# The first attention's output norm moved from VectorE to GpSimd (three of four batches), with a new order of stages

## The chip, the cores and the metric

The kernel runs on one core of a Trainium2 chip. The metric is the device time of one execution in microseconds (us). PE is TensorE, DVE is VectorE, ACT is ScalarE, POOL is GpSimd, SP is SyncE; PEld is the loading of weights into PE.

## What is computed

Three blocks in a row on an input of 4 batches, 64 channels and 32 x 32 places (1024 tokens). The first is the one that the change touches:

```
x_ln = layernorm over channels(x);  q, k, v = 4 heads of 16
attn = softmax(q k^T / 4);  out = attn v                   # 1024 x 1024 a head
x  = x + proj(out) + b
x  = x + fc2(gelu(fc1(layernorm(x))))
```

The second is an attention with 8 heads over a sliding window of 32 tokens, the third a recurrence `y = sigmoid(Wx + V y)` along the 1024 tokens behind a norm over all tokens. The three together make the result.

## The kernel before, in words

**Tiling.** A batch lies as 128 partitions (64 channels x 2 halves of 512 tokens). The first attention runs in 256 score tiles (`scores`: 4 batches, 16 units, 4 heads), each one bf16 matmul of 512 columns on PE (line 815), one exponential on ACT (line 1146) and, for every four of them, a `values` step of eight fp32 matmuls of 32 weight columns (line 830). The maximum that the softmax subtracts is found beforehand: 256 `max_piece` tiles, each one bf16 matmul on PE (line 795) and one reduction over 512 columns on DVE (line 1308). Scores and max pieces share a ring of PSUM banks (`plan_ring`): a matmul waits until ACT or DVE has read what its bank held.

**The norm.** A `values` tile carries, beside the outputs of a head, the sum of its exponentials. At the end of each half DVE copies the bank (`values`, line 1340) to `o_sb`, SP spreads the sums by DMA to `den_sb`, ACT computes `rden = exp(-log(den))` (`den`, line 1153, and `den_exp`, line 1159), and stage `o_norm` improves it by one Newton step and multiplies, in three DVE instructions a half (lines 1348, 1350 and 1352): `step = den*rden`, `step = (2 - step)*rden`, `o_norm = o_sb*step`. `proj` (line 852) on PE waits for the semaphore `o_normed` of each half, and `fc1`, `fc2`, layer norms and the whole second attention of that batch follow. The last batch (`apart`) reads its sums from PSUM and keeps buffers of its own. `o_norm` and `hid`, the hidden layer between `fc1` and `fc2`, are one buffer.

**The order.** Each engine runs its own instructions in the order of one list of stages, `order_of_stages`. The host of the list is `scores` and `values` of the four batches. `MAX_AT` says behind how many of these host stages each max piece goes, `LAYER_AT` does so (in quarter steps) for all other stages of the batches before, `END_AT` and `UNIFY_AT` for the end. So the tables set what stands ahead of what in every queue. POOL runs `split` (the parts of q and k of batches 1 to 3, which SP then sends through DRAM to the layout that scores need) and `round_query` (casts of the second attention's queries).

Of the kernel before, what the change touches and what calls it, by code (L numbers as in the profile page):

```python
# [8 lines left out]
ALU = mybir.AluOpType  # L9
# [134 lines left out]
def attend_stages(b):  # L144

    out = []
    for u in range(UNITS):
# [11 lines left out]

MAX_AT = (  # L160
    (
        0, 0, 0, 0, 1, 1, 1, 6, 6, 7, 8, 8, 10, 10, 11, 12, 13, 15, 15, 15, 15, 16, 21, 21, 21, 21, 21, 22, 24, 29, 34),
    (
        39, 39, 39, 39, 46, 46, 48, 48, 49, 51, 51, 51, 53, 55, 55, 55, 58, 59, 60, 61, 61, 63, 63, 68, 68, 68, 68,
        71, 71, 73, 74, 76, 76, 79, 79),
    (
        80, 80, 80, 83, 83, 83, 84, 85, 86, 86, 86, 86, 98, 99, 100, 101, 101, 101, 101, 103, 105, 105, 105, 105, 105,
        106, 107, 107, 107, 107, 107, 107, 109, 110, 112),
    (
        112, 114, 114, 116, 116, 116, 116, 117, 117, 117, 118, 119, 120, 122, 122, 125, 125, 127, 127, 136, 136, 137,  # L170
        137, 137, 137, 138, 143, 143, 146, 146, 147, 147, 147, 149, 151),
    (
        154, 155, 157, 157, 160, 163, 163, 163, 164, 167, 168, 169, 170, 171, 172, 172, 172, 181, 181, 185, 185, 185,
        185, 185, 186, 186, 187, 188, 188, 188, 189, 190, 190, 191, 191),
    (
        191, 193, 194, 196, 196, 196, 196, 197, 197, 197, 197, 198, 198, 198, 198, 198, 202, 208, 216, 221, 221, 221,
        222, 222, 222, 223, 223, 224, 224, 229, 229, 232, 233, 234, 234),
    (
        234, 237, 237, 239, 239, 240, 240, 242, 242, 242, 243, 243, 244, 254, 255, 255, 255, 257, 257, 257, 258, 258,
        260, 261, 261, 262, 262, 262, 266, 266, 267, 268, 271, 271, 271),  # L180
)
LAYER_AT = (
# [72 lines left out]
def build(nc, a, out):  # L255

    with ExitStack() as ctx:
        def sb(name, shape, dt=F32):
            return ctx.enter_context(nc.sbuf_tensor(name, shape, dt))

        def sem(name):
            return ctx.enter_context(nc.semaphore(name))
# [15 lines left out]
        for n in ("w1q", "w1k", "w1v", "w1u"):  # L278
# [45 lines left out]
        o_sb = sb("o_sb", [P, 2, HALF])  # L324
# [3 lines left out]
        o_norm = sb("o_norm", [P, 2, HALF])  # L328
# [50 lines left out]
            ln_ctr ln_sq ln_var ln_log ln_rstd ln_norm  # L379
            bias_mm bias_done fold_mm fold_done qk_mm v_mm qk_hi qk_rst qk_mid qk_lo qk_dram qk_in v_copied  # L380
            max_mm max_red negmax negmax_t mx_h mx_r mx_m mx_done shift_in
            st_mm exp_done pv_mm o_copied den_in den_mm den_log rden_done den_prod rden_new o_normed proj_mm x1_done
            fc1_mm gelu_done fc2_mm x2_done
            xp_pad xbd_cast z_mm z_copied z_moved z_cast z_cast_odd tok_mm tok_copied
            sel_zero sel_done lay_mm lay_in lay_in2
# [5 lines left out]
        g = {n: sem(n) for n in names}  # L391


        def half_rows(h):
            return slice(h * C, (h + 1) * C)
# [60 lines left out]
        def pair(b):  # L456
            return T[:, 0:2, :] if apart(b) else R[:, 0:2, :]
# [184 lines left out]
        @block.gpsimd  # L642
        def _(pool):


            nc.gpsimd.memset(eps[:], 1e-5).then_inc(g["pool_fills"], 1)
            nc.gpsimd.memset(sel, 0.0).then_inc(g["sel_zero"], 1)
            for i in range(2):
                nc.gpsimd.memset(VT[i][:], 0.0).then_inc(g["pool_fills"], 1)
            pool.wait_ge(g["pool_fills"], 3)  # L650
            for i in range(2):
                nc.gpsimd.memset(VT[i][:, :, :, HD:HP], 1.0).then_inc(g["pool_fills"], 1)
            nc.gpsimd.memset(den_sb[:], 1.0)
            nc.gpsimd.memset(xp[:], 0.0)
            nc.gpsimd.memset(xbd16[:], 0.0).then_inc(g["pool_fills"], 1)
            for i in range(2):
                pool.wait_ge(g["pool_fills"], 6 + i)
                nc.gpsimd.memset(KX[i][KQ:KQ + PARTS, :, :, :], 1.0).then_inc(g["pool_fills"], 1)
            pool.wait_ge(g["pool_fills"], 8)

            def round_query(b, h):
                n = b * H1 + h
                if b == B - 1:
                    if h % 2:
                        return
                    n = b * H1 + h // 2
                pool.wait_ge(g["z_copied"], b * H1 + h + 1)
                if n:
                    pool.wait_ge(g["z_cast"], n)
                if b and h == 0:  # L670
                    pool.wait_ge(g["fin_mm"], b)
                nc.gpsimd.tensor_copy(*z_cast_of(h)).then_inc(g["z_cast"], 1)  # L672

            def split(b):
                if b == 0:
                    return
                for half in range(2):
                    pool.wait_ge(g["qk_rst"], 2 * b + half + 1)
                    nc.gpsimd.tensor_copy(mid_rows[:, half, :], qk_rest[:, half, :]).then_inc(g["qk_mid"], 1)
                for half in range(2):  # L680
                    pool.wait_ge(g["qk_mid"], 2 * b + half + 1)
                    last = nc.gpsimd.tensor_tensor(lo_rows[:, half, :], qk_rest[:, half, :], mid_rows[:, half, :], ALU.subtract)
                last.then_inc(g["qk_lo"], 1)

            run({"round_query": round_query, "split": split})
            pool.wait_ge(g["unit_sel_done"], 1)
            nc.gpsimd.memset(v_cross, 0.0).then_inc(g["cross_zero"], 1)
            pool.wait_ge(g["cross_zero"], 1)
            nc.gpsimd.tensor_copy(v_cross[half_rows(0), half_rows(1)], t["v_rec"][half_rows(0), half_rows(0)]).then_inc(g["cross_done"], 1)
# [562 lines left out]
        def _(dve):  # L1252
# [88 lines left out]

            def o_norm_(b, half):

                if half == 0:
                    dve.wait_ge(g["rden_done"], b + 1)
                n = 2 * b + half + 1
                _, first, step = (x[:, half, :] for x in recip_bufs(b))
                TT(step, dens(b)[:, half, :], first, ALU.mult).then_inc(g["den_prod"], 1)
                dve.wait_ge(g["den_prod"], n)
                STT(step, step, 2.0, first, ALU.subtract, ALU.mult, reverse0=True).then_inc(g["rden_new"], 1)  # L1350
                dve.wait_ge(g["rden_new"], n)
                TT(o_norm[:, half, :], o_sb[:, half, :], step, ALU.mult).then_inc(g["o_normed"], 1)
# [266 lines left out]
```

## Time and profile before

| | us |
|---|---|
| median of 3 runs | 460.96 |
| lowest, highest | 454.33, 461.22 |
| the profiled execution | 458.44 |
| its span, first to last instruction | 456.5 |
| PE busy | 413.2 |
| DVE busy, ACT busy | 296.7, 296.3 |
| POOL busy | 42.3 |

The time of the profiled execution has 1.94 us around its span. Busy time is a union over an engine's instructions; that of PE is modelled from pipelined matmuls and so stands above its true use.

### The profile page before, as it was taken

What the parts mean: (1) busy time and instruction counts of PE and PEld (TensorE: products, weight loads), DVE (VectorE), ACT (ScalarE), POOL (GpSimd) and SP (SyncE); (2) the same over time, 40 slices, a digit from 0 to 9 for tenths busy, and PEclk for the clock granted to TensorE, in tenths of its full rate; (3) what the DMA queues carried; (4) which work ended last, traced back from release to release, by engine and by line L of the source; (5) the groups of instructions that cost most, each with busy time, mean ns of one, the idle gap of its engine ahead of it and who ended that gap; (6) DMA issues with size and microseconds to landing.
All of it is one profiled execution on the core that took longest, in us unless ns stands there. A gap on an engine that the chain in (4) does not pass through costs nothing.

```text
span 456.5 us, 7908 instructions
## 1 busy us (share of the span) xinstructions
PE 413.2 (91%) x3210; PEld 156.6 (34%) x3210; DVE 296.7 (65%) x541; ACT 296.3 (65%) x512; POOL 42.3 (9%) x57
## 2 busy tenths in 40 slices
PE   6787999999999999999999999899999988897893
PEld 2335232322322433232224433232134322453492
DVE  1696795989998746579885556997042644625424
ACT  3442577758788477587876675779977756264551
POOL 9300110003003000012031000000300000100000
PEclk9997699999999999999999999999999999799997
DMA  7300065001810000005500000000000000000003
GB/s 294 99 1 1 3 130 79 12 2 23 183 16 1 14 1 1 1 13 128 81 3 13 1 1 3 12 2 1 1 3 1 0 1 0 3 1 2 1 1 93
DMA packets 7158, 14.02 MB, mean 31 GB/s; under 512 B 1872, under 2 KB 4176, under 8 KB 6992
## 3 DMA queue, kind: packets, MB, share of 16 engines
q1 hardware_dynamic: 7120, 13.50, 12.7%
q8 instruction: 26, 0.43, 0.4%
q14 instruction: 12, 0.10, 0.1%
HBM read 9.20 MB, written 3.41 MB: 28 GB/s over the span
## 4 chain that ended last, share of the span: by engine, by line
PE 63%; ACT 15%; DVE 13%; issue 3%; DMA 3%; POOL 2%; SPq 1%; DVEq 0%; ACTq 0%; POOLq 0%
PE O L830 10%; PE T L815 5%; DVE part_max L1308 5%; PE T L795 5%; ACT z L1169 4%; PE R L815 3%; PE R L727 3%; PE R L999 3%; PE R L886 3%; PE R L795 3%; PE R L960 3%; PE R L721 2%; PE R L987 2%; DMA KX<-qk_scratch 2%; PE R L974 2%
## 5 line engine op out<-in xcount | busy, mean ns | idle before, releaser
L1308 DVE TENSOR_REDUCE part_max<-T 128x1 f32<-128x512 f32 x164 | 105.7, 683 | 23.4 <-PE T L795 23.1
L1146 ACT ACTIVATE probs<-T 128x512 f32<-128x512 f32 x146 | 81.3, 601 | 23.4 <-PE T L815 23.1
L1146 ACT ACTIVATE probs<-R 128x512 f32<-128x512 f32 x110 | 62.2, 599 | 19.2 <-PE R L815 18.9
L830 PE MATMUL O<-probs,VT 128*32 128x512 f32 x512 | 67.6, 603 | 0.3 <-ACT probs L1146 0.2
L1308 DVE TENSOR_REDUCE part_max<-R 128x1 f32<-128x512 f32 x92 | 60.7, 683 | 10.0 <-PE R L795 9.5
L795 PE MATMUL T<-KX,QX 96*128 96x512 bf16 x164 | 57.0, 393 | 4.6 <-DVE part_max L1308 3.0
L815 PE MATMUL T<-QX,KX 99*128 99x512 bf16 x146 | 49.6, 384 | 1.8 <-DVE part_max L1308 1.3
L815 PE MATMUL R<-QX,KX 99*128 99x512 bf16 x110 | 38.1, 382 | 0.6 <-DVE qk_rest L1285 0.4
L672 POOL CAST zs<-z 128x512 bf16<-128x512 f32 x28 | 17.2, 614 | 200.6 <-ACT z L1169 200.6
L795 PE MATMUL R<-KX,QX 96*128 96x512 bf16 x92 | 32.7, 387 | 1.8 <-DMA KX<-qk_scratch 0.9
L1177 ACT ACTIVATE p<-R 128x1024 f32<-128x1024 f32 x14 | 14.3, 1024 | 26.7 <-PE R L960 26.7
L795 PEld LDWEIGHTS T<-KX,QX 96*128 96x128 bf16 x164 | 15.0, 99 | 47.8 <-DVE part_max L1308 18.6
L1169 ACT ACTIVATE z<-R 64x512 f32<-64x512 f32 (+1 forms) x44 | 26.2, 596 | 5.6 <-PE R L886 4.6
L815 PEld LDWEIGHTS T<-QX,KX 99*128 99x128 bf16 x146 | 12.6, 97 | 38.1 <-ACT probs L1146 12.5
L1430 DVE TENSOR_TENSOR zs<-R,rden 128x512 f32<-128x512 f32 x24 | 15.4, 685 | 13.4 <-PE R L987 13.4
L1104 ACT ACTIVATE ln_q<-R 128x512 f32<-128x512 f32 (+1 forms) x14 | 8.2, 589 | 20.6 <-PE R L721 20.6
L886 PE MATMUL R<-xp,abd 64*64 64x512 f32 x128 | 17.2, 613 | 2.4 <-ACT z L1169 2.1
L1184 ACT ACTIVATE rlog<-R 128x1024 f32<-128x1024 f32 x16 | 16.3, 1020 | 4.7 <-PE R L974 4.6
L830 PEld LDWEIGHTS O<-probs,VT 128*32 128x32 f32 x512 | 10.3, 108 | 26.4 <-issue 15.8
L1400 DVE TENSOR_REDUCE neg_m<-R 128x16 f32<-128x576 f32 x16 | 12.1, 758 | 10.5 <-PE R L921 10.5
L815 PEld LDWEIGHTS R<-QX,KX 99*128 99x128 bf16 x110 | 9.7, 97 | 24.5 <-issue 6.4
L727 PE MATMUL R<-ln_q,s_first 128*128 128x512 f32 (+1 forms) x28 | 16.1, 660 | 2.1 <-ACT ln_q L1104 2.1
(241 smaller groups left out, 592.8 us busy)
## 6 DMA issues: line engine op xcount, KB each, us to landing
qk_scratch<-qk_part SPq DMA_DIRECT2D x12, 192.0 KB, 3.0
zs<-early SPq DMA_DIRECT2D x1, 2048.0 KB, 8.4
QX<-qk_scratch SPq DMA_DIRECT2D x6, 256.0 KB, 5.4
KX<-qk_scratch SPq DMA_DIRECT2D x6, 256.0 KB, 5.7
result<-probs SPq DMA_DIRECT2D x2, 512.0 KB, 5.1
s_rest<-rest SPq DMA_DIRECT2D x1, 946.0 KB, 11.1
X<-x SPq DMA_DIRECT2D x2, 384.0 KB, 12.6
QX<-qk_scratch SPq DMA_DIRECT2D x6, 128.0 KB, 5.5
```

Source lines behind the costliest of these rows:

```text
L672: nc.gpsimd.tensor_copy(*z_cast_of(h)).then_inc(g["z_cast"], 1)
L727: mm(ln_bank(b, which, i, 1), t["mean_c"], ln_bufs(b, which, i)["ln_q"], start=True, stop=True).then_inc(g["ln_var"], 1)
L795: mm(ring["max_piece", b, half, i], QX[b % 2][0:KQ, half, h, nt * P:(nt + 1) * P], KX[b % 2][0:KQ, kh, h, :], start=True, stop=True).then_ ...
L815: mm(ring["scores", b, u, h], KX[b % 2][:, j // QT, h, j % QT * P:(j % QT + 1) * P], QX[b % 2][:, half, h, :], start=True, stop=True).then ...
L830: last = mm(O[h * HP:(h + 1) * HP, :], VT[b % 2][:, j, h, :], probs[:, u % 2, h, :], start=(j == 0), stop=(j == KT - 1))
L886: last = mm(R[half_rows(half ^ odd), (h + odd) % z_banks(b), :], abd[half_rows(half), h + odd, half_rows(half)], xn[half_rows(half), :], s ...
L1146: A(probs[:, u % 2, h, :], ring["scores", b, u, h], ACT.Exp, scale=HD ** -0.5).then_inc(g["exp_done"], 1)
L1169: last = A(dst, ps, ACT.Copy)
L1177: A(p1[:, r % 2, :, :], s1_bank(b, r), ACT.Exp).then_inc(g["p1_exp"], 1)
L1184: A(rlog[:, :, :], den1_bank(b, r), ACT.Ln).then_inc(g["den1_log"], 1)
L1308: nc.vector.tensor_reduce(part_max[:, row, kh:kh + 1], ring["max_piece", b, half, i], AX_X, ALU.max).then_inc(g["max_red"], 1)
L1430: last = TT(cols, pv1_bank(b, r)[odd].rearrange("p (k h q) -> p k h q", k=PPS, h=H1), rden1(b, r)[:, odd, :].rearrange("p (k h q) -> p k h ...
```

## The change

In batches 0 to 2 the stage `o_norm` leaves DVE's stream and is done by POOL. [...] The first half waits for ACT's `rden_done`, and from batch 1 on for `fc2_mm` of the batch before, since `hid` shares the buffer. All four tables of places are new. In the diff the first `o_norm_` is POOL's, the second DVE's.

```diff
+            def o_norm_(b, half):
+                if apart(b):
+                    return
+                n = 2 * b + half + 1
+                if half == 0:
+                    pool.wait_ge(g["rden_done"], b + 1)
+                    if b:
+                        pool.wait_ge(g["fc2_mm"], b)
+                _, first, step = (x[:, half, :] for x in recip_bufs(b))
+                nc.gpsimd.tensor_tensor(step, dens(b)[:, half, :], first, ALU.mult).then_inc(g["den_prod"], 1)
+                pool.wait_ge(g["den_prod"], n)
+                nc.gpsimd.tensor_scalar(step, step, -1.0, 2.0, ALU.mult, ALU.add).then_inc(g["den_rest"], 1)
+                pool.wait_ge(g["den_rest"], n)
+                nc.gpsimd.tensor_tensor(step, step, first, ALU.mult).then_inc(g["rden_new"], 1)
+                pool.wait_ge(g["rden_new"], n)
+                nc.gpsimd.tensor_tensor(o_norm[:, half, :], o_sb[:, half, :], step, ALU.mult).then_inc(g["o_normed"], 1)
...
-            run({"round_query": round_query, "split": split})
+            run({"round_query": round_query, "o_norm": o_norm_, "split": split})
...
             def o_norm_(b, half):
 
+                if not apart(b):
+                    return
                 if half == 0:
                     dve.wait_ge(g["rden_done"], b + 1)
```

Written out with the tables, the order of stages differs in these places (the number is how many of the 256 `scores` stand ahead):

| stage | before | after |
|---|---|---|
| `project` of batch 1, 2, 3 | 1, 67, 136 | 2, 68, 131 |
| `den_exp` of batch 0, 1, 2 | 70, 139, 195 | 71, 134, 197 |
| `proj` of batch 0, 1, 2 | 80, 148, 205 | 84, 144, 208 |
| `queries` 0 of batch 0, 1, 2 | 92, 158, 222 | 96, 157, 224 |
| `unify` of batch 0, 1 | 122, 189 | 122, 191 |

Between `den_exp` and `proj` there now stand 13 scores, 13 max pieces and 3 `values` in batch 0; 10, 13 and 2 in batch 1; 11, 12 and 3 in batch 2. Behind the 256th score the same stages are left in both, in nearly the same order.

## Rows read from the trace of the kernel before

**Rows 1.** The page: span, part 1, and part 2's slices of DVE
```profile
span 456.5 us, 7908 instructions
...
PE 413.2 (91%) x3210; PEld 156.6 (34%) x3210; DVE 296.7 (65%) x541; ACT 296.3 (65%) x512; POOL 42.3 (9%) x57
...
DVE  1696795989998746579885556997042644625424
```
**Rows 2.** Stretches: length; busy us of PE, PEld, DVE, ACT, POOL; clock
```profile
65.00:340.00 275.00, 264.15 (x1969) 84.24 (x1961) 201.72 (x361) 205.51 (x346) 21.66 (x32) 1.00 0.14 27
100.00:130.00 30.00, 28.17 (x131) 8.59 (x124) 28.41 (x49) 23.07 (x38) 3.46 (x4) 1.00 0.42 84
207.00:222.00 15.00, 14.36 (x70) 3.84 (x62) 14.16 (x23) 11.88 (x20) 0.74 (x1) 1.00 0.75 155
290.00:310.00 20.00, 18.74 (x85) 5.36 (x87) 19.37 (x31) 16.79 (x28) 0.00 (x0) 1.00 0.02 5
340.00:456.00 116.00, 96.78 (x961) 50.53 (x960) 50.74 (x103) 61.89 (x104) 2.83 (x6) 0.95 0.04 10
```
**Rows 3.** Waits of PE (for whom: us in total, times, longest us)
```profile
PE T L795 <- DVE part_max L1308: 3.0, 12, 0.4
...
PE T L815 <- DVE part_max L1308: 1.3, 3, 0.7
...
PE R L795 <- DMA KX<-qk_scratch: 0.9, 1, 0.9
```
**Rows 4.** DVE by line and shape, the whole run (xcount, busy us, mean ns)
```profile
L1352 DVE TENSOR_TENSOR o_norm<-o_sb,rstep 128x512 f32<-128x512 f32 x6 | 4.2, 693 | 0.2
L1350 DVE SCALAR_TENSOR_TENSOR rstep<-rstep,rden 128x512 f32<-128x512 f32 x6 | 4.2, 692 | 0.2
...
L1348 DVE TENSOR_TENSOR rstep<-den_sb,rden 128x512 f32<-128x512 f32 x6 | 4.1, 685 | 0.3 <-ACT rden L1159 0.3
```
**Rows 5.** POOL by line and shape, the whole run
```profile
L672 POOL CAST zs<-z 128x512 bf16<-128x512 f32 x28 | 17.2, 614 | 200.6 <-ACT z L1169 200.6
...
L682 POOL TENSOR_TENSOR qk_part<-qk_rest,qk_part 128x512 bf16<-128x512 f32 x6 | 6.8, 1158 | 0.0
```
**Rows 6.** Timeline, 230 us: a query's copies on ACT, its cast on POOL
```profile
230.27 1.82 ACT L1169 ACTIVATE z<-R 128x512 f32<-128x512 f32 x3
...
230.94 0.61 POOL L672 CAST zs<-z 128x512 bf16<-128x512 f32 x1 [23.19 <-ACT z L1169]
```
**Rows 7.** The chain that ended last: steps from matmul to matmul
```profile
192.19 1.85 PE O L830 x16
...
195.48 0.43 PE T L815 x2
```
**Rows 8.** Timeline, 110 us: POOL's products, and three reductions in a row on DVE
```profile
109.85 2.28 POOL L682 TENSOR_TENSOR qk_part<-qk_rest,qk_part 128x512 bf16<-128x512 f32 x2
...
110.92 1.88 DVE L1308 TENSOR_REDUCE part_max<-T 128x1 f32<-128x512 f32 x3
```
**Rows 9.** Timeline around the norm of batch 2: ACT, DVE, PE
```profile
293.40 1.06 ACT L1159 ACTIVATE rden<-rlog 128x1024 f32<-128x1024 f32 x1
...
298.35 0.69 DVE L1352 TENSOR_TENSOR o_norm<-o_sb,rstep 128x512 f32<-128x512 f32 x1
...
299.03 1.13 PE L852 MATMUL R<-o_norm,s_rest 128*64 128x512 f32 x4
```
**Rows 10.** Timeline at 136 us and line 1372 of DVE (ns min/median/max)
```profile
135.83 1.23 DVE L1372 CAST xbd<-xp 64x544 bf16<-64x544 f32 x2
136.15 0.61 POOL L672 CAST zs<-z 128x512 bf16<-128x512 f32 x1 [24.03 <-ACT z L1169]
...
L1372 DVE CAST xbd<-xp x8: 426/438/787, 135.8 to 385.8; 64x544 bf16<-64x544 f32 x8
```
**Rows 11.** Timeline, 52 us: ACT and PE around `project` of batch 1
```profile
52.13 0.60 ACT L1146 ACTIVATE probs<-T 128x512 f32<-128x512 f32 x1 [0.78 <-PE T L815]
...
53.64 1.27 ACT L1122 ACTIVATE qk_part<-R,qk_bias 128x512 bf16<-128x512 f32 x2 [0.92 <-PE R L741]
```

More of the change, by code:

```diff
@@ L161 @@
     (
-        0, 0, 0, 0, 1, 1, 1, 6, 6, 7, 8, 8, 10, 10, 11, 12, 13, 15, 15, 15, 15, 16, 21, 21, 21, 21, 21, 22, 24, 29, 34),
+        0, 0, 1, 1, 1, 4, 4, 4, 5, 5, 5, 5, 7, 10, 10, 11, 11, 14, 15, 15, 17, 17, 18, 22, 22, 23, 23, 25, 25, 29, 39),
     (
-        39, 39, 39, 39, 46, 46, 48, 48, 49, 51, 51, 51, 53, 55, 55, 55, 58, 59, 60, 61, 61, 63, 63, 68, 68, 68, 68,
-        71, 71, 73, 74, 76, 76, 79, 79),
-    (
-        80, 80, 80, 83, 83, 83, 84, 85, 86, 86, 86, 86, 98, 99, 100, 101, 101, 101, 101, 103, 105, 105, 105, 105, 105,
-        106, 107, 107, 107, 107, 107, 107, 109, 110, 112),
@@ L169 @@
-    (
-        112, 114, 114, 116, 116, 116, 116, 117, 117, 117, 118, 119, 120, 122, 122, 125, 125, 127, 127, 136, 136, 137,
-        137, 137, 137, 138, 143, 143, 146, 146, 147, 147, 147, 149, 151),
-    (
-        154, 155, 157, 157, 160, 163, 163, 163, 164, 167, 168, 169, 170, 171, 172, 172, 172, 181, 181, 185, 185, 185,
-        185, 185, 186, 186, 187, 188, 188, 188, 189, 190, 190, 191, 191),
-    (
-        191, 193, 194, 196, 196, 196, 196, 197, 197, 197, 197, 198, 198, 198, 198, 198, 202, 208, 216, 221, 221, 221,
-        222, 222, 222, 223, 223, 224, 224, 229, 229, 232, 233, 234, 234),
@@ L178 @@
-    (
-        234, 237, 237, 239, 239, 240, 240, 242, 242, 242, 243, 243, 244, 254, 255, 255, 255, 257, 257, 257, 258, 258,
-        260, 261, 261, 262, 262, 262, 266, 266, 267, 268, 271, 271, 271),
+        39, 39, 39, 43, 45, 45, 45, 46, 51, 52, 53, 53, 53, 55, 58, 58, 58, 58, 62, 63, 63, 65, 65, 66, 66, 66, 70,
+        70, 71, 73, 73, 76, 78, 79, 79),
+    (
+        80, 80, 80, 83, 83, 87, 87, 87, 87, 87, 87, 88, 90, 91, 91, 92, 95, 96, 98, 98, 101, 104, 105, 106, 106, 106,
+        107, 107, 108, 108, 108, 108, 108, 111, 112),
@@ new lines @@
+    (
+        112, 112, 112, 112, 115, 116, 122, 124, 124, 124, 124, 124, 126, 126, 127, 127, 130, 131, 131, 131, 134, 136,
+        139, 139, 139, 139, 139, 139, 141, 143, 143, 146, 147, 147, 148),
+    (
+        150, 150, 150, 151, 153, 155, 156, 158, 158, 158, 159, 159, 159, 162, 162, 164, 165, 166, 166, 166, 166, 166,
+        168, 168, 170, 171, 172, 172, 173, 175, 175, 175, 175, 179, 179),
+    (
+        189, 189, 189, 189, 189, 190, 195, 195, 195, 196, 196, 197, 197, 197, 197, 197, 198, 198, 198, 199, 201, 212,
+        219, 219, 219, 219, 219, 224, 229, 229, 229, 230, 230, 234, 235),
@@ L181 @@
+    (
+        240, 240, 240, 241, 242, 242, 243, 243, 244, 245, 245, 246, 250, 251, 253, 253, 253, 253, 258, 259, 259, 260,
+        261, 262, 263, 263, 265, 266, 266, 266, 269, 270, 272, 273, 277),
 )
 LAYER_AT = (
[10 rows of a table removed]
[10 rows of a table added]
 )
 END_AT = (
-    214, 214, 216, 217, 220, 221, 223, 223, 226, 227, 227, 228, 229, 231, 231,
+    214, 216, 219, 219, 220, 221, 223, 223, 226, 227, 227, 228, 229, 230, 231,
 )
 UNIFY_AT = (
-    277, 278, 278, 278, 282, 283, 283, 285, 286,
+    278, 278, 278, 278, 281, 281, 282, 285, 286,
@@ L381, in build @@
             max_mm max_red negmax negmax_t mx_h mx_r mx_m mx_done shift_in
-            st_mm exp_done pv_mm o_copied den_in den_mm den_log rden_done den_prod rden_new o_normed proj_mm x1_done
+            st_mm exp_done pv_mm o_copied den_in den_mm den_log rden_done den_prod den_rest rden_new o_normed proj_mm x1_done
             fc1_mm gelu_done fc2_mm x2_done
```

20 rows, old and new, of the table LAYER_AT are left out of this document.

## The prediction

> **What bounds the kernel now.** I read part 1 and the slices first: PE is busy 91% of the span, DVE and ACT 65% each, POOL 9% [rows 1]. The average hides that DVE's slices swing from 4 tenths to 9. So the second view is busy time by stretch [rows 2]. From 65 to 340 us, where the scores of three batches run with everything else between them, PE is busy 264.15 of 275 us at full clock, so 10.85 us are idle. This is the stage that the change works on, and PE's queue bounds it. Three stretches of it hold the output norms of batches 0, 1 and 2. In them DVE is the busiest: 28.41 of 30, 14.16 of 15 and 19.37 of 20 us, 94 to 97%, while PE stands at 28.17, 14.36 and 18.74. PE lacks 1.83 + 0.64 + 1.26 = 3.73 us there. The third view, the waits of PE, agrees on the cause: banks of the ring that DVE has not reduced yet cost it 3.0 us before max pieces and 1.3 us before scores [rows 3]. From 340 us on (116 us, DVE busy 50.74) the kernel is a chain of short steps, and DVE is not what lacks.
>
> **What leaves DVE.** Three batches by two halves by three instructions are 18, of 685, 692 and 693 ns [rows 4]: 6 x 2.07 = 12.4 us, 4.14 us a batch, all inside the three stretches. With that gone DVE's share there falls from about 95% to about 76% (61.9 of 65 us less 12.4), and ACT with 51.7 of 65 us is level with it. The relief can return at most what PE idles. For it I take 3.7 us, the idle time of the three stretches. The bounds are nothing (PE's gaps pass to ACT) and 10.85 us (the new order fills every gap of the stage).
>
> **What comes on POOL.** Four instructions a half. POOL's product of two tiles of 512 columns took 1158 ns, with one fp32 and one bf16 operand and a bf16 result [rows 5]; the change's products are fp32 throughout, a form that the trace doesn't show. The tensor_scalar it doesn't show either; a cast of 512 columns took 614 ns, the other one-input row. I take 1158 and 614: if POOL counts elements rather than bytes, that is the price. The lower bound for the product is the same 1158, since nothing in it is smaller; the upper one is 1158 x 12/8 = 1737 ns, if bytes set the pace (4 + 2 in and 2 out against 4 + 4 and 4). The tensor_scalar lies between 614 and 1158. A handoff costs 0.07 us: the cast of 230.94 begins that long behind the first of ACT's three copies, of 0.60 us each, which began at 230.27 [rows 6]. A batch then takes 2 x (3 x 1.158 + 0.614) + 8 x 0.07 = 8.7 us from `rden` to the second `o_normed`, against 4.2 us on DVE. With the upper bounds it is 2 x (3 x 1.737 + 1.158) + 0.56 = 13.3 us.
>
> The Trainium skill, GPSIMD Engine Reference, section Performance versus the Vector engine, speaks against the move: it calls POOL about twice as slow for two-input work, and gives 4497 ns for an fp32 sum of 2048 columns. A quarter of it, 1124 ns, is an estimate for 512 fp32 columns, and a batch would be 8.5 us by it. The trace's own ratio is 1158 to 685.
>
> **What covers it.** Nobody but `proj` needs `o_norm`, so the 8.7 us are free if PE has that much to do ahead of it. Before, the placement left no margin: `rden` of batch 2 ended at 294.46, DVE's last product at 299.04, and PE began `proj` at 299.03, its second half some 0.5 us later [rows 9]. The new list puts 13 scores, 13 max pieces and 3 `values` between `den_exp` and `proj` in batch 0. In the chain a score or max piece takes PE 0.215 us and a `values` 0.93 us [rows 7], which makes 26 x 0.215 + 3 x 0.93 = 8.4 us. Batch 1 has 23 x 0.215 + 2 x 0.93 = 6.8 us on PE; its 13 reductions hold the ring for 13 x 0.60 = 7.8 us, as three in a row took 1.88 [rows 8]. Batch 2 has 23 x 0.215 + 3 x 0.93 = 7.7 us. PE is never quite full, and its second half of `proj` is needed 0.5 us later, which adds some 0.8 us to each; PE runs about as much ahead of ACT. So 8.7 us against 8.4, 7.8 and 7.7 leaves PE waits of 0.3, 0.9 and 1.0 us, less what margin the idle gives. I take 1.0 us in all, between 0 and 2.2. If that cover were gone entirely, the price would be the added 4.5 us a batch.
>
> **POOL's own queue.** Behind the waiting product stand `split` of the next batch and the casts of queries. `round_query` of batch 0 comes 15 scores behind the norm, and the casts wait for ACT anyway (200.6 us of idle before them [rows 5]). `split` of batch 3 now stands ahead of batch 1's norm with 3 scores between its `project` and it; POOL has 3.5 us of `split` (two casts, two products [rows 5]), which end while ACT still does `den` and `den_exp`. DVE's copy into `o_sb` at the middle of the next batch newly waits for POOL, but stands 16 scores behind `proj`. The wait on `fc2_mm` is long met. SP's queue keeps its order. These I cost at nothing.
>
> **Two moves beside it.** `project` of batch 1 has one more exponential (0.60 us) ahead on ACT, which idles 0.92 us before it [rows 11]. It feeds the transfers of which PE already waits 0.9 us [rows 3], so I take 0.3 us of loss (0 to 0.6). The order behind the last score is nearly the same: nothing, give or take 0.5.
>
> **The sum.** 458.4 for the profiled execution, less 3.7, plus 1.0, plus 0.3, is 456.0 us. That execution lies 2.5 us under the median of the three runs and 4.1 us over the lowest, so the runs scatter by more than the effect; the mean of all four is 458.7. I predict 457 us for a median, a little above the sum.
>
> **The rivals.** (a) *No gain.* The idle time in the stretches passes from DVE to ACT or to the layer norm's chain, and only the 1.3 us of cost remain: 459.7. For it: ACT stands at 79% there, and only 4.3 us of PE's waits name DVE's reductions. Against: DVE at 94 to 97% exactly there.
> (b) *A larger gain.* The new order uses the freed DVE time in the whole stage, 8 of the 10.85 us: 458.4 - 8 + 1.3 = 451.7, the edge of 2%. For it: 12.4 us of DVE are freed. Against: outside the stretches DVE has been idle anyway.
> (c) *Slower: POOL becomes what `proj` waits for.* At 13.3 us a batch PE waits 13.3 - 8.4 = 4.9, 5.5 and 5.6 us, 16 us in all: 458.4 - 3.7 + 16.3 = 471. It decides from some 9 us a batch on, where each further 0.1 us per product costs 6 x 3 x 0.1 = 1.8 us; for 2% slower it needs products of 1.55 us or more. Against: the trace's product moves 8 bytes an element where its cast moves 6, and takes 1.9 times as long, so it is rather the second operand that costs.
> (d) *A shared port.* The trace shows DVE and POOL holding each other up: the second cast of line 1372 at 136 us took 787 ns where the median is 438, just while POOL's cast of 136.15 to 136.76 ran [rows 10]. POOL's 24 new instructions would hold up DVE's casts and two-input steps for up to 1.16 us each. In the stretches most of DVE's work is reductions from PSUM, and those took the same 0.60 us a step with POOL's products beside them [rows 8]; a handful of steps of the maxima's parts remain, so 3 us at most: 459.
> The Trainium skill, SBUF — State Buffer, section Who interferes with whom, states the rule behind (d): the pair of ports is locked for a whole instruction, against DVE's two-input and two-port forms alone, never its reductions. By this rule the trace agrees.
>
> **How the numbers follow.** Forecast 0.50, (a) 0.22, (b) 0.12, (c) 0.07, (d) 0.09. Two per cent is 9.2 us, about what this kernel's measurement can tell. Faster by more needs (b) and a low run: 0.10. Slower by more needs (c): 0.06. Within: 0.84. The range reaches from 450.5 (under (b), by half the scatter) to 464 (above (a) and (d), with the runs' scatter, without the far end of (c)).
>
> **What the profile after would show.** DVE near 284 us busy with 18 instructions less, POOL near 67; POOL's products at 1.16 us; DVE's share in the norm stretches near 80%; PE's idle time between 65 and 340 us down to about 8 us; waits of PE's `proj` on POOL under 1 us each. Products over 1.5 us, a wait of several us before `proj`, or PE's idle time unchanged would prove the sum wrong.

## The result, and the profile after

The change made the kernel slower: a median of 471.3 us (467.4 to 475.5) against 461.1 us for the kernel before, a ratio of 1.030 with a 95% interval of 1.024 to 1.036. The ratio compares executions in the faster of two states (the plain quotient of the medians is 1.022), and the profiled execution after is of the slower one. It took 475.5 us, 4 us over the median, and it spent 2.6 us more than the kernel before behind the last score, where the two have the same work.

The page of the kernel after (compare [rows 1]) and its busy time by stretch, in the columns of [rows 2]:

```profile
span 473.7 us, 7915 instructions
...
PE 421.9 (89%) x3209; PEld 158.5 (33%) x3210; DVE 285.3 (60%) x523; ACT 297.0 (63%) x512; POOL 68.9 (15%) x81
...
65.00:362.00 297.00, 278.05 (x2056) 88.20 (x2055) 193.20 (x350) 211.16 (x355) 48.17 (x56) 0.99 0.13 25
213.00:223.00 10.00, 7.77 (x36) 2.11 (x37) 7.02 (x14) 5.44 (x11) 8.82 (x8) 1.00 0.80 168
223.00:226.00 3.00, 3.00 (x11) 0.35 (x10) 0.75 (x1) 0.00 (x0) 0.00 (x0) 0.52 1.03 188
```

VectorE lost 11.4 us and GpSimd gained 26.6, as the change says. But in the score stage, where PE was idle for 10.85 us before, it is now idle for 297.00 - 278.05 = 18.95 us. (The window is longer because the last score now begins at 361.7 us; it began at 347.1, and counted to there PE was idle for 10.86 us before.) In the ten microseconds around the norm of batch 1 all of PE, DVE and ACT have gaps, and only POOL is full; in the three behind them the granted clock is 0.52, the lower of TensorE's two levels (1.2 of 2.4 GHz).

GpSimd's work by line and shape in the kernel after (compare [rows 4, 5]), and who PE waited for (compare [rows 3]):

```profile
L683 POOL TENSOR_TENSOR rstep<-den_sb,rden 128x512 f32<-128x512 f32 x6 | 7.6, 1274 | 53.7 <-ACT rden L1176 53.7
L687 POOL TENSOR_TENSOR rstep<-rstep,rden 128x512 f32<-128x512 f32 x6 | 7.6, 1268 | 0.5
L689 POOL TENSOR_TENSOR o_norm<-o_sb,rstep 128x512 f32<-128x512 f32 x6 | 7.6, 1268 | 0.5
...
L685 POOL TENSOR_SCALAR rstep<-rstep 128x512 f32<-128x512 f32 x6 | 3.7, 621 | 0.5
...
PE R L869 <- POOL o_norm L689: 4.7, 3, 2.2
PE R L744 <- ACT ln_q L1121: 3.7, 6, 1.9
...
PE T L812 <- DVE part_max L1325: 2.5, 11, 0.3
```

The waits for VectorE's reductions are hardly shorter (3.0 before, 2.5 after). A new one stands at the top: three waits of `proj` (now line 869) for POOL. The timeline shows which half it is. First POOL in batch 0, first and last instruction, then PE's `proj` in batches 0, 1 and 2 with what follows it in batch 1:

```profile
112.51 1.27 POOL L683 TENSOR_TENSOR rstep<-den_sb,rden 128x512 f32<-128x512 f32 x1 [0.44 <-ACT rden L1176]
...
120.56 1.26 POOL L689 TENSOR_TENSOR o_norm<-o_sb,rstep 128x512 f32<-128x512 f32 x1
...
119.65 1.07 PE L869 MATMUL R<-o_norm,s_rest 128*64 128x512 f32 x2
121.88 1.07 PE L869 MATMUL R<-o_norm,s_rest 128*64 128x512 f32 x2 [1.16 <-POOL o_norm L689]
...
219.28 1.07 PE L869 MATMUL R<-o_norm,s_rest 128*64 128x512 f32 x2
222.58 1.47 PE L869 MATMUL R<-o_norm,s_rest 128*64 128x512 f32 x2 [2.23 <-POOL o_norm L689]
223.98 1.94 PE L847 MATMUL O<-probs,VT 128*32 128x512 f32 x8
...
314.21 1.07 PE L869 MATMUL R<-o_norm,s_rest 128*64 128x512 f32 x2
316.62 1.07 PE L869 MATMUL R<-o_norm,s_rest 128*64 128x512 f32 x2 [1.33 <-POOL o_norm L689]
```

The norm of batch 0 runs from 112.51 to 121.82 on POOL, 9.3 us. PE begins the first half of `proj` at 119.65, when it has been ready for 2.5 us, and then stands before the second. Where nothing waits, the two halves run side by side: before, the four matmuls of both took 1.13 us [rows 9], and here two of them, one half alone, take 1.07. So every us that the second half begins behind the first is a us lost. It comes 2.23, 3.30 and 2.41 us behind, 7.9 us in all. The rows call only 4.7 us of it idle, since PE counts as busy with the first half alone. Behind the longest wait the clock is at the lower level, and a `values` step takes 1.94 us where it takes 1.06 elsewhere.

### The profile page after: what moved, and what is told of

Same layout as the page of the kernel before. It is cut to its first block, busy times and chain, and to the rows that moved or that the text cites. A ratio compares the mean times of both kernels' runs of the same rounds, so it can differ in the third digit from the quotient of the medians.

```text
span 473.7 us, 7915 instructions
## 1 busy us (share of the span) xinstructions
PE 421.9 (89%) x3209; PEld 158.5 (33%) x3210; DVE 285.3 (60%) x523; ACT 297.0 (63%) x512; POOL 68.9 (15%) x81
## 4 chain that ended last, share of the span: by engine, by line
PE 59%; ACT 17%; DVE 12%; POOL 7%; issue 3%; DMA 1%; SPq 1%; DVEq 0%; POOLq 0%; ACTq 0%
PE O L847 8%; PE T L832 4%; DVE part_max L1325 4%; ACT z L1186 4%; PE T L812 4%; PE R L832 3%; PE R L744 3%; PE R L1016 3%; PE R L738 3%; PE R L977 3%; PE R L903 3%; PE R L812 2%; PE R L1004 2%; PE R L991 2%; PE R L938 2%
## 5 line engine op out<-in xcount | busy, mean ns | idle before, releaser
L1325 DVE TENSOR_REDUCE part_max<-T 128x1 f32<-128x512 f32 x162 | 104.4, 681 | 23.1 <-PE T L812 22.8
L1163 ACT ACTIVATE probs<-T 128x512 f32<-128x512 f32 x151 | 83.8, 599 | 20.5 <-PE T L832 19.9
L1163 ACT ACTIVATE probs<-R 128x512 f32<-128x512 f32 x105 | 59.5, 599 | 24.3 <-PE R L832 23.9
L1325 DVE TENSOR_REDUCE part_max<-R 128x1 f32<-128x512 f32 x94 | 62.1, 682 | 14.8 <-PE R L812 14.4
L812 PE MATMUL T<-KX,QX 96*128 96x512 bf16 x162 | 55.5, 394 | 3.9 <-DVE part_max L1325 2.5
L832 PE MATMUL R<-QX,KX 99*128 99x512 bf16 x105 | 36.5, 386 | 0.5 <-DVE part_max L1325 0.2
L696 POOL CAST qk_part<-qk_rest 128x512 bf16<-128x512 f32 x6 | 3.7, 615 | 146.8 <-DVE qk_rest L1302 146.7
## 6 DMA issues: line engine op xcount, KB each, us to landing
s_rest<-rest SPq DMA_DIRECT2D x1, 946.0 KB, 10.2
```

What stands on the lines that cost most here:

```text
L812: mm(ring["max_piece", b, half, i], QX[b % 2][0:KQ, half, h, nt * P:(nt + 1) * P], KX[b % 2][0:KQ, kh, h, :], start=True, stop=True).then_ ...
L832: mm(ring["scores", b, u, h], KX[b % 2][:, j // QT, h, j % QT * P:(j % QT + 1) * P], QX[b % 2][:, half, h, :], start=True, stop=True).then ...
L1163: A(probs[:, u % 2, h, :], ring["scores", b, u, h], ACT.Exp, scale=HD ** -0.5).then_inc(g["exp_done"], 1)
L1325: nc.vector.tensor_reduce(part_max[:, row, kh:kh + 1], ring["max_piece", b, half, i], AX_X, ALU.max).then_inc(g["max_red"], 1)
```

## The experiments

The stage from the 65th to the 256th score matmul is compared below beside the timed ratios. It begins between 101.3 and 105.6 us in all kernels, and leaves out start and tail. The stage is of the profiled execution, the ratio of the timed ones.

| kernel | norm in batches 0 to 2 | places | 65th to 256th score, us | ratio to before |
|---|---|---|---|---|
| before | DVE, 4.2 us | old | 243.3 | 1 |
| e7 | POOL, one product, 2.5 us | old | 244.8 | 0.999 (0.995 to 1.003) |
| e6 | a half on each | old | 247.9 | 1.012 (1.006 to 1.018) |
| e2 | POOL, 9.3 us | old | 264.5 | 1.043 (1.034 to 1.051) |
| e9 | POOL, 9.3 us | old, proj and its layers later | 294.4 | 1.108 (1.099 to 1.117) |
| e4 | POOL, one product, 2.5 us | new | 248.5 | 1.010 (1.005 to 1.015) |
| e16 | POOL, two products, 5.2 us | new | 248.5 | 1.016 (1.008 to 1.024) |
| the change | POOL, 9.3 us | new | 257.9 | 1.030 (1.024 to 1.036) |
| e10 | the change, proj's wait filled | new | 255.9 | 1.023 (1.016 to 1.031) |
| e13 | the change, proj later | new, shifted | 257.3 | 1.032 (1.026 to 1.037) |
| e5 | a half on each | new | 262.0 | 1.041 (1.030 to 1.052) |
| e1 | DVE | new | 264.5 | 1.049 (1.038 to 1.059) |
| e11 | as e4 | new, then old | 261.4 | 1.039 (1.032 to 1.047) |
| e12 | as e4 | old, then new | 264.2 | 1.045 (1.039 to 1.052) |

**Engine against places.** e1 takes the kernel before and gives it the new tables; e2 takes the change and gives it the old ones. The first row of `MAX_AT` in e1 stands for all of it (`MAX_AT`, `LAYER_AT`, `END_AT`, `UNIFY_AT`); e2 has the reverse:

```diff
-        0, 0, 0, 0, 1, 1, 1, 6, 6, 7, 8, 8, 10, 10, 11, 12, 13, 15, 15, 15, 15, 16, 21, 21, 21, 21, 21, 22, 24, 29, 34),
+        0, 0, 1, 1, 1, 4, 4, 4, 5, 5, 5, 5, 7, 10, 10, 11, 11, 14, 15, 15, 17, 17, 18, 22, 22, 23, 23, 25, 25, 29, 39),
```

> The norm stays on VectorE in all batches, with the new places. Theory L (latency): the loss is PE's wait for GpSimd's 9.3 us of norm before proj (4.7 us seen by the profile, and what is late behind it), so without it the time is that of before or a little more: ratio 0.99 to 1.01, no wait of PE for o_norm. Theory P (places): the new order by itself loses, since it bunches max pieces and puts stages of layer norms in a row, so the ratio stays at 1.02 to 1.03 with the waits for o_norm gone.

> The norm on GpSimd as in the change, with the places of before. The old order has PE at proj 4.3 to 4.6 us behind rden, and GpSimd takes 9.3 us. Theory L: PE waits 4.5 to 5 us for o_norm in each of three batches, 14 us in all, ratio 1.025 to 1.035. Theory P: the wait is filled in by what is queued behind, ratio at most 1.01.

e1 took 480.4 us and e2 477.5: either half of the change alone is worse than both. So neither theory holds by itself, and both runs lie outside what both theories gave. In e2 latency does what theory L says, and more. PE's waits for `o_norm` are the longest entry, and the first of them, with the clock behind it:

```profile
PE R L869 <- POOL o_norm L689: 11.8, 6, 3.5
...
116.90 1.04 PE L869 MATMUL R<-o_norm,s_rest 128*64 128x512 f32 x2 [0.54 <-POOL o_norm L689]
121.41 1.97 PE L869 MATMUL R<-o_norm,s_rest 128*64 128x512 f32 x2 [3.47 <-POOL o_norm L689]
...
121.00:127.00 6.00, 5.59 (x9) 1.69 (x10) 2.73 (x4) 1.19 (x2) 0.36 (x1) 0.50 0.88 140
```

The clock falls in or behind the wait in each of the three batches. The expected 4.5 to 5 us of wait a batch were about right; the falls come on top. In e1 another mechanism is at work. Theory P named the bunched max pieces, but not that the norm stands in front of them. DVE and PE of e1 in batch 1, and the clock behind:

```profile
212.08 0.69 DVE L1348 TENSOR_TENSOR rstep<-den_sb,rden 128x512 f32<-128x512 f32 x1
...
215.58 0.69 DVE L1352 TENSOR_TENSOR o_norm<-o_sb,rstep 128x512 f32<-128x512 f32 x1
216.19 1.28 DVE L1308 TENSOR_REDUCE part_max<-T 128x1 f32<-128x512 f32 x2
...
213.37 0.38 PE L815 MATMUL R<-QX,KX 99*128 99x512 bf16 x1
216.93 0.41 PE L795 MATMUL T<-KX,QX 96*128 96x512 bf16 x1 [3.18 <-DVE part_max L1308]
...
217.00:223.00 6.00, 5.81 (x18) 1.29 (x19) 3.86 (x7) 1.79 (x3) 0.00 (x0) 0.51 1.02 185
```

The new places put a run of max pieces right behind `o_norm`. With the norm in DVE's queue, 4.2 us of it stand ahead of those reductions, the ring fills up, PE stands still for 3.18 us, and its clock falls. In batch 2 it stands for 4.22 us (from 306.07 to 310.29), again until a reduction is done. The new order needs VectorE free there: the two parts of the change belong together.

**Latency taken away.** e4 is the change with the first three of POOL's four instructions a half left out:

```diff
-                nc.gpsimd.tensor_tensor(step, dens(b)[:, half, :], first, ALU.mult).then_inc(g["den_prod"], 1)
-                pool.wait_ge(g["den_prod"], n)
-                nc.gpsimd.tensor_scalar(step, step, -1.0, 2.0, ALU.mult, ALU.add).then_inc(g["den_rest"], 1)
-                pool.wait_ge(g["den_rest"], n)
-                nc.gpsimd.tensor_tensor(step, step, first, ALU.mult).then_inc(g["rden_new"], 1)
-                pool.wait_ge(g["rden_new"], n)
-                nc.gpsimd.tensor_tensor(o_norm[:, half, :], o_sb[:, half, :], step, ALU.mult).then_inc(g["o_normed"], 1)
+                nc.gpsimd.tensor_tensor(o_norm[:, half, :], o_sb[:, half, :], first, ALU.mult).then_inc(g["o_normed"], 1)
```

> The new places, and GpSimd does only the last product of each half in batches 0 to 2, 1.27 us instead of 4.65: the Newton step of the reciprocal is left out there. DVE keeps being relieved of all 18 instructions. Theory L: proj has its input 2.6 us behind rden, no wait of PE for it, ratio 0.985 to 1.00 (some 14 us less than the change). Theory P: 1.01 to 1.025, as PE then waits for other things in the same stretches.

It took 462.3 us, ratio 1.010. PE in batch 1, where the change waited longest:

```profile
215.23 1.08 PE L863 MATMUL R<-o_norm,s_rest 128*64 128x512 f32 x4
216.24 1.07 PE L841 MATMUL O<-probs,VT 128*32 128x512 f32 x8
```

Both halves of `proj` run in one piece, and the clock doesn't fall in the score stage. Of the loss, 9.0 us are gone (471.3 to 462.3). But a per cent of loss stays, at the lower edge of what theory P gave (1.01 to 1.025) and above what L allowed, although VectorE is relieved of all 18 instructions.

The two traces can be laid side by side, since both kernels have the same order: from the 65th score on, PE starts each score at the same distance as in e4, to 0.03 us, but for three places. At the 85th, 145th and 209th score, the first ones behind `proj`, the change falls back by 2.23, 4.84 and 2.40 us. That is the 9.5 us between 248.5 and 257.9. The waits of the second half are 2.2, 3.3 and 2.4 us of it, and what is left, 1.5 us in batch 1, lies where the clock is at the lower level for 3.4 us.

e16 puts one unused product back (`step = den*rden`, ahead of the last), for 5.2 us a batch (POOL, 111.50 to 116.69 in batch 0):

```diff
-                nc.gpsimd.tensor_tensor(step, dens(b)[:, half, :], first, ALU.mult).then_inc(g["den_prod"], 1)
-                pool.wait_ge(g["den_prod"], n)
-                nc.gpsimd.tensor_scalar(step, step, -1.0, 2.0, ALU.mult, ALU.add).then_inc(g["den_rest"], 1)
+                nc.gpsimd.tensor_tensor(step, dens(b)[:, half, :], first, ALU.mult).then_inc(g["den_rest"], 1)
                 pool.wait_ge(g["den_rest"], n)
-                nc.gpsimd.tensor_tensor(step, step, first, ALU.mult).then_inc(g["rden_new"], 1)
-                pool.wait_ge(g["rden_new"], n)
-                nc.gpsimd.tensor_tensor(o_norm[:, half, :], o_sb[:, half, :], step, ALU.mult).then_inc(g["o_normed"], 1)
+                nc.gpsimd.tensor_tensor(o_norm[:, half, :], o_sb[:, half, :], first, ALU.mult).then_inc(g["o_normed"], 1)
```

> New places; GpSimd does two products a half, of which the first (den times rden) is not used, and the second is the product with o_sb, so its part takes some 5.4 us a batch, between the 2.6 us of the kernel with one product (462.3 us, ratio 1.010) and the 9.3 of the change (471.3, 1.030). The Newton step of the reciprocal is left out in batches 0 to 2. In the change PE arrived at proj 6.2 to 7.2 us behind rden. Theory L (a threshold, PE's arrival at proj): nothing is late, 461 to 464 us, ratio 1.005 to 1.015. Theory M' (each us of latency is paid, wherever proj stands): 2.8 of 6.7 us more, 465 to 467, ratio 1.017 to 1.022.

Its `proj` in batch 0 has both halves in one piece:

```profile
118.64 1.08 PE L865 MATMUL R<-o_norm,s_rest 128*64 128x512 f32 x4
```

Its score stage takes 248.5 us, to the tenth that of e4, though the norm takes twice as long, and score by score the two differ by 0.03 us at most. The timed ratio, 1.016, has too wide an interval (1.008 to 1.024) to tell the two theories apart; the trace does. PE reached `proj` 7.2, 5.8 and 7.0 us behind the end of `rden`, and 5.2 us of latency cost nothing, while 9.3 us cost 9.5. It is a threshold, between these two.

**The same with the old places, and the port.** e7 is e4 with the tables of before. e6 is e2 with half 0 left on DVE and half 1 on POOL, at the same time, with semaphores for each half; e5 is the same with the new tables. The core of it, ahead of the four instructions on POOL and the three on VectorE:

```diff
-                if apart(b):
+                if apart(b) or half != 1:
                     return
...
-                if not apart(b):
+                if not apart(b) and half == 1:
                     return
...
-                    pe.wait_ge(g["o_normed"], 2 * b + half + 1)
+                    pe.wait_ge(g["o_normed%d" % half], b + 1)
```

> GpSimd does only the last product of each half (the Newton step of the reciprocal is left out in batches 0 to 2), with the places of before. Against the same kernel with the new places, which took 462.3 us, it gives the price of the new places without the latency. Theory P (the new order costs on its own): 454 to 458 us, 4 us or more below it. If the order is neutral: 460 to 464. And against before it gives what 12.4 us off VectorE are worth: theory R 3.7 us (ratio 0.992), or nothing (1.00).

e7 took 457.7 us, ratio 0.999 (0.995 to 1.003). It answers the first question of the prediction: 11.7 us off VectorE, with no latency added, are worth nothing. The same three stretches as in [rows 2], taken 2 us earlier since e7 began its scores 1.5 us earlier:

```profile
98.00:128.00 30.00, 28.17 (x130) 8.36 (x127) 24.66 (x43) 23.07 (x38) 5.96 (x6) 1.00 0.42 84
205.00:220.00 15.00, 14.38 (x70) 3.84 (x62) 10.33 (x17) 11.89 (x20) 3.47 (x3) 1.00 0.74 153
288.00:308.00 20.00, 18.66 (x74) 5.17 (x75) 13.97 (x24) 15.38 (x26) 2.50 (x2) 0.91 0.03 6
```

VectorE fell from 28.41, 14.16 and 19.37 us to 24.66, 10.33 and 13.97. PE stands at 28.17, 14.38 and 18.66 against 28.17, 14.36 and 18.74, to a tenth the same. The waits for the reductions did not shrink either: from the 65th score to the last they are 1.5 and 1.3 us in both kernels (before max pieces and before scores). In batch 2 one of them can be seen before and in e7, with what follows it:

```profile
293.79 0.39 PE L815 MATMUL T<-QX,KX 99*128 99x512 bf16 x1 [0.73 <-DVE part_max L1308]
...
295.31 1.07 PE L830 MATMUL O<-probs,VT 128*32 128x512 f32 x8
```

```profile
292.02 0.39 PE L826 MATMUL T<-QX,KX 99*128 99x512 bf16 x1 [0.73 <-DVE part_max L1319]
...
293.54 1.66 PE L841 MATMUL O<-probs,VT 128*32 128x512 f32 x8
```

The wait is the same, and before it ends ahead of the norm, which begins at 294.85. So reductions do hold PE up, but the norm is not what holds up these reductions. The `values` step shows something else: behind the same waits the clock was at the lower level from 293.9 us on for 3.4 us in e7, and not before. Up to there the two kernels start their scores within 0.16 us of each other (counted from the 65th), and over that fall e7 loses 1.6 us. That is all of the 1.5 us by which its stage is longer, so without the fall the relief is worth 0 to 0.2 us.

And 462.3 less 457.7 is the price of the new places with a short norm, 4.6 us (3.7 us in the score stage, or 5.2 against the kernel before, whose stage has no fall of the clock either). PE waits for ACT's squares of the layer norms 3.0 us in e4 and 1.9 in e7, and for the copies of queries 3.1 and 1.8.

> One half of the norm on each engine (VectorE 2.1 us, GpSimd 4.7 us at the same time), with the places of before. Proj has its input 4.7 us behind rden, where the old order has PE at 4.3 to 4.6. Theory L (the latency in front of proj decides): no PE wait over 0.5 us, no fall of TensorE's clock in the score stage, ratio 0.99 to 1.005. Theory R (any relief of VectorE is worth having): 3 to 6 us less than before, ratio below 0.995. Theory S (GpSimd beside VectorE disturbs it): ratio 1.01 or more, with VectorE's instructions longer.

> The new places; in batches 0 to 2 VectorE does half 0 of the norm (2.1 us) and GpSimd half 1 (4.65 us) at the same time, with semaphores for each half, so that proj has its input 4.7 us behind rden and not 9.3. Theory L: PE's waits for o_norm go to zero, ratio 0.99 to 1.01. Theory P: 1.015 to 1.03. Were sharing of the SBUF port what costs, VectorE's three two-input steps would run longer than 0.69 us beside GpSimd's, up to 1.3 us more each.

e6 took 464.1 us (1.012), e5 477.7 (1.041). Theory L had e6 at no loss (0.99 to 1.005), and is wrong there by what theory S named. DVE and POOL of e6 at the norm of batch 0:

```profile
114.45 1.67 DVE L1366 TENSOR_TENSOR rstep<-den_sb,rden 128x512 f32<-128x512 f32 x1
116.16 0.98 DVE L1368 SCALAR_TENSOR_TENSOR rstep<-rstep,rden 128x512 f32<-128x512 f32 x1
117.17 1.65 DVE L1370 TENSOR_TENSOR o_norm<-o_sb,rstep 128x512 f32<-128x512 f32 x1
...
114.31 1.27 POOL L682 TENSOR_TENSOR rstep<-den_sb,rden 128x512 f32<-128x512 f32 x1 [0.45 <-ACT rden L1175]
115.67 0.94 POOL L684 TENSOR_SCALAR rstep<-rstep 128x512 f32<-128x512 f32 x1
116.69 1.59 POOL L686 TENSOR_TENSOR rstep<-rstep,rden 128x512 f32<-128x512 f32 x1
118.36 1.59 POOL L688 TENSOR_TENSOR o_norm<-o_sb,rstep 128x512 f32<-128x512 f32 x1
```

VectorE's two-input steps take 1.67, 0.98 and 1.65 us where they took 0.69 alone [rows 4], and POOL's take 1.59 instead of 1.27. The first DVE step ends at 116.12, 0.54 us behind the end of POOL's product at 115.58: it was held up until then. So the two took turns, and POOL's half took 5.6 us (114.31 to 119.95) where its four instructions alone take 4.7, and VectorE's 4.4 us where it takes 2.1 alone. The Trainium skill, SBUF — State Buffer, section Who interferes with whom, states this lock for DVE instructions with two SBUF inputs beside a GpSimd instruction that reads SBUF. By this rule the trace agrees. In the change itself it plays no part: its products took 1262 to 1282 ns, the same throughout, as VectorE then had only reductions beside them.

What e6 loses against e7 is again latency in front of `proj`. Score by score it falls back in two places of the stage, by 1.47 us behind `proj` of batch 0 and by 1.66 behind that of batch 1. Its `proj` in these two batches:

```profile
118.97 2.10 PE L868 MATMUL R<-o_norm,s_rest 128*64 128x512 f32 x4 [0.38 <-DVE o_norm L1370]
...
215.45 1.07 PE L868 MATMUL R<-o_norm,s_rest 128*64 128x512 f32 x2
217.12 1.07 PE L868 MATMUL R<-o_norm,s_rest 128*64 128x512 f32 x2 [0.60 <-POOL o_norm L688]
```

POOL's half was done 5.7 and 5.9 us behind `rden`, where PE arrives at 4.3 us in the old order. Shared evenly but side by side, the work comes too late by what the two hold each other up. e5 has the new order, and its loss is like that of e1: VectorE's half, 4.3 us long in batch 1, stands ahead of a run of reductions, and PE stands still for 3.32 us in batch 1 and 5.45 in batch 2:

```profile
219.14 0.61 PE L811 MATMUL T<-KX,QX 96*128 96x512 bf16 x1 [3.32 <-DVE part_max L1324]
```

Both theories had e5 lower (at most 1.03).

**Filling or moving the wait.** e10 puts six bf16 matmuls into rows that the second half overwrites, between the halves of `proj`:

```diff
                 for half in range(2):
+                    if half and not apart(b):
+                        for _ in range(6):
+                            mm(single(b)[half_rows(1), :], ones16[:, 0:C], ones16[:, 0:512], start=True, stop=True)
                     pe.wait_ge(g["o_normed"], 2 * b + half + 1)
```

> The change with six bf16 matmuls of 512 columns, 1.3 us, between the two halves of proj in batches 0 to 2, where PE waits 1.2 to 2.2 us for GpSimd's second half; they write rows that the second half overwrites. Theory K (the fall of TensorE's clock behind that wait is a part of the price): no stretch at half clock at 223 us, and the time 2 to 4 us below the change's, 467 to 469. If the clock fall has other causes or no price: same time as the change or 0.5 us more, half clock at 223 us as before.

It took 469.5 us, ratio 1.023 (1.016 to 1.031) beside the change's 1.030; theory K had 467 to 469. The wait is still there, the fall of the clock is not:

```profile
220.62 1.07 PE L872 MATMUL R<-o_norm,s_rest 128*64 128x512 f32 x2 [1.26 <-POOL o_norm L689]
...
221.00:227.00 6.00, 5.75 (x28) 1.47 (x26) 1.94 (x5) 2.60 (x5) 0.00 (x0) 1.00 0.84 134
```

The score stage is 2.1 us shorter than the change's, and all of it is gained at one place, the 145th score, behind `proj` of batch 1. Of it 0.55 us are not the clock's: `rden` ended that much earlier beside PE's own work (PE came to `proj` 6.70 us behind it, and 6.15 in the change). So the fall costs 1.5 us, the same as in the comparisons above. The timed intervals overlap and don't show it. That this fall came of the wait is likely and not shown: with the wait shorter (here) or nearly gone (e13, below) it is absent, but that is one trace each, and e7 and e6 have a fall of 3.4 us in batch 2 with no wait over 0.73 us in the 8 us ahead of it.

e13 moves `proj` of each batch 10 quarter places later and the eight layer entries behind it by 9, 8, 6, 5, 4, 3, 2 and 1. e9 does the like to the old tables, by 24 quarter places falling to none over 40 entries.

In e13 the entries 415, 417, 419, 425, 428, 434, 437, 450 and 450 of `LAYER_AT` became 425, 426, 427, 431, 433, 438, 440, 452 and 452 in batch 0, 715, 717, 717, 727 and on became 725, 726, 726, 733 and on in batch 1, and likewise in batch 2.

> The change as it is, full norm on GpSimd, with proj of batches 0 to 2 moved 2.5 host stages (some 1.6 us of PE work) later and the eight layer stages behind it by less and less. In the change PE's second half of proj began 1.7, 2.8 and 1.9 us behind its own place in the queue. Theory L: two thirds of that is filled, no half clock at 223 us, 465 to 468 us instead of 471.3. Theory M (what is filled is paid again as the layer norms behind proj come closer together): 470 to 473, with longer waits of PE for ACT's squares and of layer stages for each other.

> The whole norm on GpSimd, places of before, but proj of batches 0 to 2 moved 6 host stages (about 5 scores) later, and the layer stages behind it by less and less. With the places of before as they are this norm took 477.5 us. Theory L: the 5 us of cover remove the waits and the falls of the clock in the score stage, 457 to 464 us. If it is GpSimd's work itself that costs, the time stays above 470.

e13 took 472.0 us, ratio 1.032: nothing gained. The clock doesn't fall in its score stage. Who PE waited for in e13, and its `proj` in batch 1:

```profile
PE R L732 <- ACT ln_q L1109: 5.6, 9, 1.9
PE R L891 <- ACT z L1174: 3.1, 8, 0.5
...
219.30 1.07 PE L857 MATMUL R<-o_norm,s_rest 128*64 128x512 f32 x2
220.75 1.07 PE L857 MATMUL R<-o_norm,s_rest 128*64 128x512 f32 x2 [0.37 <-POOL o_norm L677]
```

The wait for `o_norm` is down to 0.37 us, in batch 1 alone, and the wait for the squares of the layer norms has grown from 3.7 to 5.6 us. The chain behind `proj` (layer norm, fc1, fc2, layer norm) became as much tighter as `proj` became later. Theory M's forecast came true. e9 is the same mistake in large: 507.7 us. PE's waits for the copies of queries are 11.2 us, ten of them, and between the 65th and 256th score there are seven stretches at the lower clock.

```profile
PE R L904 <- ACT z L1187: 11.2, 10, 1.9
...
137.00:144.00 7.00, 5.78 (x14) 1.38 (x14) 1.82 (x4) 2.60 (x6) 0.00 (x0) 0.56 0.01 2
```

My shift had pushed the stages behind `proj` together: `queries` 2 to 7 of batch 0, which have the places 464 to 477 in the old table, stand at 478, 481 and 486 in e9, two at each. So e9 doesn't test theory L, and what it shows is that a bunched order costs more than the latency it covers.

**Where the price of the places lies.** e11 and e12 are e4 with the tables cut. In e11 the first three rows of `MAX_AT` (host places up to 112, max pieces of scores up to 90) and the first 85 entries of `LAYER_AT` (up to batch 0's `wx`, score 128) are the new ones, and everything behind is old; e12 is the other way round.

> As the kernel without the Newton step (the Newton step of the reciprocal is left out in batches 0 to 2, GpSimd does one product a half), with the new places up to the end of batch 0's layers (score 128) and the old ones behind. With all old places it took 457.7 us, with all new ones 462.3. In the trace the loss stands at the seam between the layers of batch 0 and batch 1: theory P1 says that a part of it, 1 to 3 us, lies in this first third (459 to 461). Theory P0, that the 4.6 us are scatter between jobs: 457 to 458 here and in the next kernel alike.

> The complement: old places up to score 128, new ones behind; again without the Newton step in batches 0 to 2. Theory P1: the rest of the loss, 459 to 462, so that the two together give about 4.6 us over the old places. If the new order pays only as a whole (what it puts off in one part it gets back in the other), both are slower than 462.3.

They took 476.1 and 479.1 us, both far above 462.3 and 457.7. Neither P1 nor P0 fits; the third outcome on record with e12, both slower than 462.3, came about. The two tables are cut at places that don't fit each other (max pieces at score 90, layers at 128), and e11 is 9.6 us behind e4 already at its 97th score (counted from the first), where layers are still the same and max pieces are not. So the two runs don't localize the 4.6 us. They say again that parts of the two tables don't mix.

## Why the prediction was wrong, by its steps

**The sum.** It was 458.4 - 3.7 + 1.0 + 0.3, and it left the places at nothing. The runs put 0 for the relief (before to e7), 4.6 us for the places (e7 to e4), and 9.0 us for the latency (e4 to the change). As steps of one chain they add up to the whole by themselves, 13.6 us beside the 13.7 that a ratio of 1.030 makes of 458 us; the two plain medians are 10.2 us apart. The traces bear the terms out one by one: the score stage is 14.7 us longer than before (257.93 against 243.26), of which 9.5 lie at the three waits of `proj` and 5.2 are the places.

**The relief of VectorE (3.7 us forecast, 0 measured in e7).** The step that failed is the one from VectorE's 94 to 97% and PE's 3.7 us of gaps to a relief of 3.7 us. Taking 11.7 us of VectorE's work out of the run left PE's busy time in these stretches unchanged to 0.1 us. The waits of [rows 3] do name VectorE, but the 1.5 and 1.3 us of them that lie in the stage are there with the norm gone as well, so the norm isn't what stands in front of those reductions. I had rival (a) for this at 0.22; its "for" (only 4.3 us of waits name the reductions) was the better argument.

**The price on POOL (8.7 us a batch forecast, 9.3 measured).** The tensor_scalar was right (621 ns against 614), handoffs too (0.07 to 0.09 us). The fp32 products took 1268 to 1274 ns and not 1158, inside the bounds of 1158 and 1737. The estimate of 1124 ns from the figure of the Trainium skill, GPSIMD Engine Reference, section Performance versus the Vector engine, is low as well; the measured 1270 decides.

**The cover (1.0 us of waits forecast, 7.9 measured).** This is the term that was most wrong. PE reached `proj` 7.2, 6.1 and 7.0 us behind `rden`, where I had 8.4, 7.8 and 7.7. I had let PE's losses and its lead over ACT cancel. They do not: while ACT does the two long instructions of `den` and `den_exp`, PE already runs what stands behind them. Of the 26, 23 and 23 scores and max pieces of my sums only 20, 16 and 17 were still to come on PE when `rden` ended, and of the 13 reductions of batch 1 only those of 8 max pieces. That the second half is needed 0.5 us later was a misreading: the 1.13 us of [rows 9] are those of four matmuls, and before, the second half began 0.01 to 0.17 us behind the first. So what counts is the end of the whole norm, while half 0 was done 2.5, 1.4 and 2.3 us before PE came. With 9.3 against 6.1 to 7.2 the mechanism of rival (c), POOL as what `proj` waits for, was the right one, at a chance of 0.07; its threshold, "from some 9 us a batch on", was too high by 2 to 3 us.

**The clock (nothing forecast, 1.5 us measured).** In the change TensorE was at the lower level for 3.4 us behind a wait of 2.23 us, and in e2 for 3.4 to 6.8 us in each of three batches, in or behind waits of 3.5 us. The prediction priced a wait at its own length. By the comparisons with e4 and e10 the fall in the change cost 1.5 us. What brings a fall about stays open, as e7 had one behind the same waits that had none before.

**The moves of places (0.3 us forecast, 4.6 measured with a short norm).** I counted what stood ahead of `project` in batch 1 and costed the other moves at nothing. That first move may have cost its 0.3 to 0.8 us: the time from the first to the 65th score is 52.4 us before, 53.2 after and 52.9 in e4. The rest stands behind. Which of the some 500 entries make it stays open. e13 and e1 show two ways in which an order can cost, two stages of one chain of layers with too little between them, and a run of one kind of tile that one engine must clear; that these 4.6 us are of either kind is not shown.

**POOL's queue, the shared port, the tail.** That nothing queued behind POOL's waits matters held: the casts of queries are as long and no wait of PE names them newly. Rival (d) didn't occur in the change, and e6 shows that it is real where both engines do two-input steps.

## What to carry to other kernels

Before work is moved to a slower engine off the path, measure the time between the moment its input is ready and the moment its reader arrives, on the reader's own timeline, for the last part that the reader needs: within that time latency cost nothing (e16), and 2.2, 3.3 and 2.4 us beyond it cost 9.5 us, 1.5 of them through the clock. Where two kernels have the same order, subtract the starts of one engine's instructions, one by one: the places where the difference jumps are where the time goes. A busy share of 95% is no proof that relief is worth something, and neither are waits that name the engine; take the work away in one experiment first (e7). In a kernel whose order is laid out by hand, work and places have to be changed together, and each of them alone can be worse than both (e1, e2).

## What the runs showed of the hardware

- In the change GpSimd's product of two fp32 tiles of 128 x 512 into fp32 took 1262 to 1282 ns, against 1158 with one bf16 input and a bf16 result; its tensor_scalar took 621.
- In e6 VectorE's two-input steps on SBUF beside GpSimd's took up to 1.67 us instead of 0.69, and GpSimd's products up to 1.79 instead of 1.27. A half on each took 5.6 to 5.9 us side by side, where one behind the other they are 4.7 + 2.1 = 6.8, and VectorE alone takes 4.2 for both.
- TensorE's granted clock was at its lower level for 3.4 us behind a wait of 2.23 us in the change, for 6.8, 6.8 and 3.4 us in or behind waits of 3.5 us in e2, and not at all behind one of 1.26 us in e10. In e7 it was there for 3.4 us behind waits of 0.73, 0.21 and 0.21 us, and before, behind the same three waits, it was not. A fall of 3.4 us cost 1.5 to 1.6 us.
- The two halves of `proj`, which write different halves of the partitions, ran side by side on PE: four matmuls in 1.08 us (e4), where two, one half alone, took 1.07 (the change).
